# Cross-attention maxima of a two-layer Perceiver kernel: from full-array matmuls to pairs in the two row halves of the array

## The reference

```python
# layer 0: 8 heads of 64, queries from layernorm(x), keys and values from the context
scores = jnp.einsum('bhnd,bhmd->bhnm', q, k) * 64 ** -0.5
out = jnp.einsum('bhnm,bhmd->bhnd', softmax(scores), v)
x = x + out.reshape(b, n, 512) @ Wo + bo

# layer 1: 16 heads of 16, with biases
energy = jnp.einsum('bhqd,bhkd->bhqk', Q, K) / 4
x = x + einsum(softmax(energy), V).reshape(B, S, 256) @ wo.T + bo
```

## Time and profile before

| | us |
|---|---|
| median of 3 runs | 1888.92 (1888.12 to 1889.22) |
| the profiled execution | 1879.97, its span 1878.3 |
| PE busy | 1603.4 (85%) |
| PE weight loads busy | 1193.4 (64%) |
| DVE busy | 1122.9 (60%) |
| ACT busy | 790.6 (42%) |
| POOL busy | 500.8 (27%) |

### The profile page before, as it was taken

How to read it: one execution, slowest core, us unless ns; L and a number is a source line. 1 busy time by engine, 2 the same in 40 slices (tenths; PEclk the granted TensorE clock), 3 DMA queues, 4 the chain that set the end, 5 groups by cost and what they waited for, 6 DMA issues and landing times. The chain is left out here.

```text
span 1878.3 us, 26909 instructions
## 1 busy us (share of the span) xinstructions
PE 1603.4 (85%) x10311; PEld 1193.4 (64%) x10311; DVE 1122.9 (60%) x1784; ACT 790.6 (42%) x1084; POOL 500.8 (27%) x630
## 2 busy tenths in 40 slices
PE   5989999999999668779997787998999899875299
PEld 3777777777777457558887564555665555433288
DVE  3976666666652465356665798777666777005641
ACT  3545555555544132224442223555555555651110
POOL 0004434434469000000000202444333544640000
PEclk9999999999999877679999999999999899997599
DMA  2122212212222100022221110110010010000253
GB/s 79 57 57 68 66 48 68 65 49 68 57 57 46 34 1 1 22 92 81 77 95 38 34 46 23 35 35 24 23 35 23 25 33 12 1 1 23 90 170 110
DMA packets 75443, 92.35 MB, mean 49 GB/s; under 512 B 7442, under 2 KB 62276, under 8 KB 75332
## 3 DMA queue, kind: packets, MB, share of 16 engines
q1 hardware_dynamic: 75140, 90.79, 16.3%
q10 hardware_dynamic: 192, 0.05, 0.0%
HBM read 73.47 MB, written 0.52 MB: 39 GB/s over the span
## 5 line engine op out<-in xcount | busy, mean ns | idle before, releaser
L591 POOL CAST st<-ef 32x512 fp32r<-32x512 f32 x384 | 233.5, 608 | 369.2 <-PE score L1173 325.6
L1744 DVE TENSOR_REDUCE mx<-bank 128x1 f32<-128x512 f32 x384 | 246.9, 685 | 96.8 <-PE bank L1188 96.1
L777 ACT ACTIVATE P<-score 128x1024 f32<-128x1024 f32 x256 | 251.3, 1023 | 124.7 <-PE score L1173 124.6
L977 PE MATMUL bank<-c_hi,w_split 128*128 128x512 f32 x640 | 223.6, 407 | 26.1 <-DVE c_lo L1601 16.1
L1173 PE MATMUL score<-qs,st 97*128 97x512 f32 x512 | 174.1, 429 | 16.8 <-ACT P L777 11.5
L1188 PE MATMUL bank<-ef,qm 128*128 128x512 f32 x384 | 151.1, 445 | 30.1 <-DVE mx L1744 21.0
L977 PEld LDWEIGHTS bank<-c_hi,w_split 128*128 128x128 f32 x640 | 122.9, 192 | 73.6 <-issue 22.4
L556 POOL TENSOR_TENSOR sum<-sum,P 128x512 f32<-128x512 f32 x84 | 111.1, 1323 | 209.9 <-ACT P L693 209.9
L693 ACT ACTIVATE P<-score 128x1024 f32<-128x1024 f32 x128 | 130.0, 1025 | 78.5 <-PE score L1011 76.1
L977 PE MATMUL bank<-w_split,c_hi 128*128 128x256 f32 x768 | 145.7, 289 | 5.4 <-ACT v L787 5.4
L1188 PEld LDWEIGHTS bank<-ef,qm 128*128 128x128 f32 x384 | 73.1, 192 | 100.5 <-DVE mx L1744 80.5
(11 more groups left out here) (320 smaller groups left out, 2809.4 us busy)
## 6 DMA issues: line engine op xcount, KB each, us to landing
c_in<-in_ctx SPq DMA_DIRECT2D x64, 512.0 KB, 3.9
w<-k SPq DMA_DIRECT2D x128, 128.0 KB, 2.2
arena<-in_L_ffn_w SPq DMA_DIRECT2D x16, 1024.0 KB, 5.2
arena<-in_L_ffn_W SPq DMA_DIRECT2D x16, 1024.0 KB, 5.5
x<-in_x SPq DMA_DIRECT2D x1, 512.0 KB, 3.7
raw<-in_L_xattn_Wk SPq DMA_DIRECT2D x1, 512.0 KB, 6.5
raw<-in_L_xattn_Wv SPq DMA_DIRECT2D x1, 512.0 KB, 7.3
raw<-in_L_xattn_Wq SPq DMA_DIRECT2D x1, 512.0 KB, 8.2
```

The lines of the kernel that those rows point to most:

```text
L591: pool.tensor_copy(st1[32 * block:32 * block + 32, k, :], ef1[rows, g % LAG, part, :].bitcast(F32)).then_inc(a[f"st{k}"], 16)
L777: act.activation(P1[:, index % PRING, :], score[n % 2][:], ACT.Exp).then_inc(a["p"], 1)
L977: last = mm(dst, l, r, start=(n == 0), stop=(n == len(pairs) - 1))
L1744: v.tensor_reduce(mx1[:, u % 2, i, n:n + 1], bank_of(a, g + 1, f"m{n}")[:], AX.X, ALU.max).then_inc(a["red"], 1)
```

## The change

In both layers `maxima(g, h)` now takes two heads at once. Its two matmuls use 64 rows of the array each, the first rows 0 to 63 and the second rows 64 to 127 (`tile_position=(64 * j, 0)`), each for another head and the same query block, and write to the same two banks as before. In layer 0, rows hold the high key parts of the even and of the odd head of a pair, so the low parts take no part any more, and the wait is for the high keys (`kh`) instead of the low ones (`kl`). In layer 1, head h // 2 lies in the upper half and head h // 2 + 4 in the lower one. Both destinations, and with them both waits for a free bank, are asked for before the first of the two matmuls. The numbers of matmuls, reductions and semaphore steps stay the same; the reductions write their maxima to other columns of `mx0` and `mx1`, so that these hold what they held before. The wait for queries at a unit's first chunk is for the pair's heads.

```diff
 maxima(g, h), layer 0
-                        pe.wait_ge(a["qh"], a.n("qh", 8 * u + 2 * h + 2))
+                        pe.wait_ge(a["qh"], a.n("qh", 8 * u + 4 * (h // 2) + 4))
                     if h % 2 == 0:
-                        pe.wait_ge(a["kl"], a.n("kl", 2 * g + h // 2 + 1))
+                        pe.wait_ge(a["kh"], a.n("kh", 2 * g + h // 2 + 1))
                     early = g + 1 < LAG
                     if early and 4 * g + h >= 2:
                         pe.wait_ge(a["red"], a.n("red", 8 * g + 2 * h - 2))
-                    for q in range(2):
-                        dst = score[h % 2][:, 512 * q:512 * q + 512] if early else place_free(a, g + 1, f"m{2 * h + q}")[:]
-                        mm(dst, qh0[:, u % 3, h, 128 * q:128 * q + 128], k0[:, g % LAG, h, :], start=True, stop=True).then_inc(a["ms"], 1)
+                    dst = [score[h % 2][:, 512 * j:512 * j + 512] if early else place_free(a, g + 1, f"m{2 * h + j}")[:] for j in range(2)]
+                    for j in range(2):
+                        rows, head = slice(64 * j, 64 * j + 64), 2 * (h // 2) + j
+                        mm(dst[j], qh0[rows, u % 3, head, 128 * (h % 2):128 * (h % 2) + 128], k0[rows, g % LAG, head, :],
+                           start=True, stop=True, tile_position=(64 * j, 0)).then_inc(a["ms"], 1)
 maxima(g, h), layer 1
-                        pe.wait_ge(a["qh"], a.n("qh", 8 * u + h + 1))
+                        pe.wait_ge(a["qh"], a.n("qh", 8 * u + h // 2 + 5))
...
-                    for q in range(2):
-                        dst = score[h % 2][:, 512 * q:512 * q + 512] if early else place_free(a, g + 1, f"m{2 * h + q}")[:]
-                        mm(dst, qm1[:, h, 128 * q:128 * q + 128], ef1[:, g % LAG, 0, :], start=True, stop=True).then_inc(a["ms"], 1)
+                    dst = [score[h % 2][:, 512 * j:512 * j + 512] if early else place_free(a, g + 1, f"m{2 * h + j}")[:] for j in range(2)]
+                    for j in range(2):
+                        rows, q = slice(64 * j, 64 * j + 64), 128 * (h % 2)
+                        mm(dst[j], qm1[rows, h // 2 + 4 * j, q:q + 128], ef1[rows, g % LAG, 0, :],
+                           start=True, stop=True, tile_position=(64 * j, 0)).then_inc(a["ms"], 1)
 reduce(g, h), layer 0 (layer 1 alike, with col = h + 8 * j)
-                    for q in range(2):
-                        n = 2 * h + q
+                    for j in range(2):
+                        n, col = 2 * h + j, 4 * (h // 2) + h % 2 + 2 * j
                         dve.wait_ge(a["ms"], a.n("ms", 8 * g + n + 1))
-                        v.tensor_reduce(mx0[:, u % 2, i, n:n + 1], bank_of(a, g + 1, f"m{n}")[:], AX.X, ALU.max).then_inc(a["red"], 1)
+                        v.tensor_reduce(mx0[:, u % 2, i, col:col + 1], bank_of(a, g + 1, f"m{n}")[:], AX.X, ALU.max).then_inc(a["red"], 1)
```

More of the change, by code:

```diff
@@ L1601, in context_low, with reduce_early, columns0, columns1 @@
                 v.tensor_tensor(lo[:, f, :], bank_of(a, t, f"t{f}")[:], hi[:, f, :].bitcast(F32), ALU.subtract).then_inc(a["cl"], 1)
-            def reduce_early(a, mx, per_chunk, g, h):
+            def reduce_early(a, mx, per_chunk, g, h, cols):
                 dve.wait_ge(a["ms"], a.n("ms", per_chunk * g + 2 * h + 2))
-                v.tensor_reduce(mx[:, 0, g, 2 * h:2 * h + 2], score[h % 2][:].rearrange("p (q k) -> p q k", q=2), AX.X, ALU.max).then_inc(a["red"], 2)
+                v.tensor_reduce(mx[:, 0, g, cols], score[h % 2][:].rearrange("p (q k) -> p q k", q=2), AX.X, ALU.max).then_inc(a["red"], 2)
+            def columns0(h):
+                first = 4 * (h // 2) + h % 2
+                return slice(first, first + 3, 2)
+            def columns1(h):
+                return slice(h, h + 9, 8)
             def low_weights(setup, n, lo, src, hi):
@@ L1685, in cross0 @@
                         if 1 <= t < LAG:
-                            reduce_early(a, mx0, 8, t - 1, h)
+                            reduce_early(a, mx0, 8, t - 1, h, columns0(h))
                         if t < LAG and h in (1, 2):
@@ L1740, in reduce @@
                     u, i = divmod(g, NCH)
-                    for q in range(2):
-                        n = 2 * h + q
+                    for j in range(2):
+                        n, col = 2 * h + j, h + 8 * j
                         dve.wait_ge(a["ms"], a.n("ms", 16 * g + n + 1))
-                        v.tensor_reduce(mx1[:, u % 2, i, n:n + 1], bank_of(a, g + 1, f"m{n}")[:], AX.X, ALU.max).then_inc(a["red"], 1)
+                        v.tensor_reduce(mx1[:, u % 2, i, col:col + 1], bank_of(a, g + 1, f"m{n}")[:], AX.X, ALU.max).then_inc(a["red"], 1)
                 def maximum(u):
@@ L1789, in cross1 @@
                         if 1 <= t < LAG:
-                            reduce_early(a, mx1, 16, t - 1, h)
+                            reduce_early(a, mx1, 16, t - 1, h, columns1(h))
                         if t < LAG and h == 1:
```

## The result

The changed kernel takes **2004.53 us** (median of 4 runs, 2002.4 to 2006.39) against 1888.52 for the kernel before: a ratio of 1.0618, 95% interval 1.0599 to 1.0638. The forecast was slower, 1936.5 us, with a range up to 1958. The direction came true; the loss is 116 us where 47.6 were summed. The profiled execution has a span of 2001.2 us, 122.9 more than before.

What follows compares the result with a forecast made beforehand. PE alone was taken to bound layer 0, the exchange of two banks between PE and DVE layer 1. Terms 10.6 + 35 + 2 = +47.6 us gave 1927.6 profiled, plus 8.95 for the median: 1936.5 us, range 1888 to 1958.

Steps and rivals of the forecast that it cites:

- What bounds the kernel: Steady parts: PE alone in layer 0 (136.93 of 138.30 us busy); in layer 1 PE and DVE handing each other two banks.
- The change of shape: Row-half pair between full-array matmuls, priced from column tiles: 0.62 us against 0.47, so 0.15 us more.
- a visit: On PE, going into row halves and out again around a pair: 0.42 us in all, bounds nothing and 0.52.
- Rival B: Both layers: row halves need no change of shape; total about 1889 us, or 1876 with weights loaded ahead; chance 0.17.
- C: Both layers: the halves do not overlap, 1973 us; or only their weights load one after the other, 1953; chance 0.15.
- D: Layer 1: DVE hides the chain in part, giving back half that layer's sum, 1919 us; chance 0.13 for 1900 to 1925.
- Layer 0: Late chunks: PE is the bound, so costs count in full; +0.44 us per chunk, times 24 = +10.6 us.
- early chunks: Eight per layer: 0 in layer 1; in layer 0 two of four pairs stand alone between projections, +2 us.
- The chain in layer 1: Late chunks: awaiting both banks before a pair's first matmul makes pairs 1.89 us apart; +35 us in sum.
- The clock: Layer 1's loops: a fall of the granted clock would make it slower than forecast; not expected, given no size or chance.
- the two mechanisms of the forecast: Changes of array shape in layer 0's late chunks (+10.6 us) and joined waits for banks in layer 1's (+35 us).

Runs made afterwards that it cites:

- E3: Layer 0 as in the changed kernel, layer 1's maxima as in the kernel before; 1903.28 us, ratio 1.0083 to the kernel before.
- E1: Changed kernel with both banks still awaited before a pair's first matmul, but both matmuls over the full array; 1953.94 us, ratio 1.0364 to the kernel before.
- E2: Changed kernel with its row halves, but each bank awaited just before its own matmul; 1972.72 us, ratio 1.0435 to the kernel before.
- E4: Changed kernel with the scores' matmuls for n = 1 to 5 of late layer 1 chunks made twice; 1967.83 us, ratio 1.0437 to the kernel before.
- E7: E2 with the scores' matmuls for n = 1 to 5 of late layer 1 chunks made twice; 1957.38 us, ratio 1.0384 to the kernel before.
- E6: Kernel before, split waits kept, but both maxima matmuls of a head run one after the other in the same 64-row half; 2030.30 us, ratio 1.0782.
- E8: Kernel before plus a tiny 4-column tiled matmul behind late layer 1 maxima pairs, except in each unit's first mixed chunk; 1909.46 us, ratio 1.0126.

## Why the prediction was wrong

- **What bounds the kernel** was read rightly: PE alone in layer 0, the ping-pong over two banks in layer 1. E3 and E1 show each by itself.
- **The change of shape** was priced rightly from column tiles: 0.16 more for a pair between scores (0.15 forecast), 0.43 to the next instruction (0.43). What the prediction gives as 0.42 for a visit is 0.40 by its own four terms. Rival B (no change of shape for row halves) and C (no overlap) are out by the same rows, and D (the chain hidden in part) by the pairs 1.94 apart. The Trainium skill, TensorEngine Tiling (Array Packing), section Key Properties, says that a change of the tiling mode drains TensorE. The trace agrees for row tiles by the 0.16; a drain as such it does not show.
- **Layer 0**: chunks of 17.60 for 17.04, +0.56 each where 0.44 was summed; E2, with split waits, has 17.51, so some 0.1 of it is the first pair's later start. That is 13 us over 24 chunks; early chunks cost nothing (9.78 before and after) where 2 us were put down. The other 7 of the 19.9 us go with the clock, 0.97 for 0.99.
- **The chain in layer 1**: 1.94 per pair for 1.89. The matmul starts 0.14 after the reduction that frees its bank (1451.11 + 1.29 = 1452.40, matmul at 1452.54), not 0.055, and the reduction 0.51 after the matmul, not 0.54; E1 has the same 0.14 and 0.51 over the full array. In the mean a chunk at full clock (E4's, for the changed kernel has none) is about 1.9 us longer than before, where 1.45 was summed: 46 us for 35. This term was mis-sized, by nearly a third.
- **The clock** is the step that failed. The prediction named a fall of the clock in layer 1's loops and put it aside, because it had stayed at 0.96 in an early stretch with PE busy 79% of the time. PE was busy 88% of the late stretch of the changed kernel (469.02 of 534.80) and the clock was 0.78. Busy time was the wrong measure, as the late stretches of E1 and E2 show, in this order:

```profile
1167.50:1656.70 489.20, 402.63 (x2806) 251.24 (x2805) 317.14 (x501) 243.42 (x283) 187.62 (x308) 0.95 0.08 25
```

```profile
1167.80:1677.60 509.80, 480.65 (x2807) 244.26 (x2806) 316.49 (x502) 247.91 (x283) 188.08 (x307) 0.82 0.08 24
```

  E1 was busy 82% of its stretch at a clock of 0.95, E2 94% at 0.82. Busy time counts a half-array matmul as a full one, and it grows when the clock falls. What is left of the late stretch's 99.6 us after the 46, about 54, goes with the clock, together with the 7 of layer 0 some 60 us; this is a difference and not a measurement, but E4 won back 34 us of it although it has more work. It was not in the range, because no rival priced it.

So of the 122.9 us between the two spans, some 59 (46 + 13) are the two mechanisms of the forecast, and nearly all of the rest goes with the clock. That the direction came true is no luck: joined waits (E1) and row halves (E2) each make the kernel slower by themselves. The change takes away full-array work and adds waiting at once; E1 (waiting alone, 0.95) and E2 (halves alone, 0.82) each lose less than both together (0.78).

## What to carry to other kernels

A single pair of half-array matmuls side by side did not pay here: it saved 0.24 us, and the way into row halves and out again cost 0.40. By these prices runs of several pairs would pay; that is an estimate, and no run here tried it. Where two banks are handed to and fro, keep the wait for the second bank behind the first matmul. And when an edit takes matmul work out of a loop in which PE already waits, price the lower clock as a rival of its own, from a stretch of the trace that runs at it (the mixture: 3.03 us for 1.85).

## What was not expected of the hardware

- 240 needless matmuls made a kernel some 34 us faster (E4 against the changed kernel), with TensorE's granted clock at 0.95 instead of 0.78 in the late stretch. Put into E2 they brought it from 0.82 to 0.94 (E7) and made the kernel no slower.
- PE can be busier and its clock lower: 94% and 0.82 (E2), 82% and 0.95 (E1).
- Matmuls over 64 rows in row tiles held the clock up less than those over 128, at the same number of columns and nearly the same chunk: 0.85 (E6) against 0.97 (E8). Rows or mode is open.
- After a joined wait for two banks a matmul started 0.14 us after the reduction that released it (E1 and the changed kernel), after a wait for one bank some 0.05 (the kernel before and E2).
- In the changed kernel some part of every late chunk of layer 1 ran at half clock. In the one shown it fell in the loop of maxima and stood full again by the projections (0.51 from 1455.4 to 1462.3, 1.00 from there to 1472.5).
